# Causal attention with split-precision products: the scores run two tiles ahead of the transposes, and a tile's product stands behind the next tile's scores and transposes

## What is computed

```
x = x + attention(layernorm(x))
q, k, v = xn @ Wq.T, xn @ Wk.T, xn @ Wv.T               # 8 x 1024 x 256 each, one head
scores  = q @ k.T / 16, set to -inf above the diagonal
att     = softmax(scores)
attention = att @ v
```

## Time and profile before

| | |
|---|---|
| median of 3 runs | 2715.43 us (2697.62 to 2717.7) |
| the profiled execution's own time | 2705.96 us |
| span of the profile | 2703.8 us |
| the batches' tiles and projections, in the span | from 32 to 438 us, some 51 to 54 us a batch |
| busy over the span | PE 89%, PEld 82%, DVE 72%, ACT 44%, POOL 27% |

### The profile page before, as it was taken

How to read it: one execution, slowest core, us unless ns; L and a number is a source line. 1 busy time by engine, 2 the same in 40 slices (tenths; PEclk the granted TensorE clock), 3 DMA queues, 4 the chain that set the end, 5 groups by cost and what they waited for, 6 DMA issues and landing times. The chain is left out here.

```text
span 2703.8 us, 43605 instructions
## 1 busy us (share of the span) xinstructions
PE 2410.3 (89%) x15832; PEld 2204.0 (82%) x15832; DVE 1939.7 (72%) x3587; ACT 1180.7 (44%) x1834; POOL 732.7 (27%) x452
## 2 busy tenths in 40 slices
PE   6988896899899969999999999958888888799999
PEld 6887885888888858898898889847777777699998
DVE  5666665899999866467556656548999998766664
ACT  4344443434443325455456555523333333444444
POOL 1111011444444423122312302314434442211110
PEclk9999997999999989999999999968898989899999
DMA  5000000000000000000000000020000010100000
GB/s 168 0 0 0 0 0 19 1 1 0 0 0 0 1 16 1 16 8 8 16 12 8 12 16 8 9 67 24 17 24 16 16 39 2 41 19 21 23 23 32
DMA packets 43112, 45.91 MB, mean 17 GB/s; under 512 B 2976, under 2 KB 42016, under 8 KB 42784
## 3 DMA queue, kind: packets, MB, share of 16 engines
q1 hardware_dynamic: 43040, 44.95, 5.2%
HBM read 28.16 MB, written 16.78 MB: 17 GB/s over the span
## 5 line engine op out<-in xcount | busy, mean ns | idle before, releaser
L1777 ACT ACTIVATE m_a<-m_ps_wide,m_b 128x512 f32<-128x512 f32 x128 | 88.4, 690 | 286.3 <-PE m_ps_wide L271 202.1
L1745 PE MATMUL m_ps_z<-m_w_hi,m_a_hi 128*128 128x256 f32 x512 | 152.9, 299 | 52.8 <-DVE m_a_lo L1817 52.8
L1777 ACT ACTIVATE d_a<-d_ps_wide,d_b 128x512 f32<-128x512 f32 x128 | 88.3, 690 | 190.4 <-PE d_ps_wide L271 188.4
L1817 DVE TENSOR_TENSOR d_a_lo<-d_a,d_a_hi 128x512 fp32r<-128x512 f32 x128 | 86.8, 690 | 111.3 <-ACT d_a_hi L1781 110.4
L1269 POOL TENSOR_TENSOR p_kf<-p_kf,p_k_shift 128x1024 f32<-128x1024 f32 x64 | 119.5, 1904 | 155.3 <-DVE p_k_shift L1403 155.3
L1745 PEld LDWEIGHTS m_ps_z<-m_w_hi,m_a_hi 128*128 128x128 f32 x512 | 103.2, 202 | 66.7 <-DVE m_a_lo L1817 61.7
L1745 PE MATMUL m_ps_z<-m_w_lo,m_a_hi 128*128 128x256 f32 x512 | 150.1, 293 | 0.0
L1745 PE MATMUL m_ps_z<-m_w_hi,m_a_lo 128*128 128x256 f32 x512 | 149.9, 293 | 0.0
L1745 PE MATMUL d_ps_z<-d_w_hi,d_a_lo 128*128 128x256 f32 x512 | 145.4, 284 | 0.0
L1745 PE MATMUL d_ps_z<-d_w_lo,d_a_hi 128*128 128x256 f32 x512 | 145.0, 283 | 0.0
L1745 PE MATMUL d_ps_z<-d_w_hi,d_a_hi 128*128 128x256 f32 x512 | 143.9, 281 | 0.3 <-DVE d_a_lo L1817 0.3
(11 more groups left out here) (342 smaller groups left out, 8567.6 us busy)
## 6 DMA issues: line engine op xcount, KB each, us to landing
residual<-in_x SPq DMA_DIRECT2D x8, 1024.0 KB, 11.8
attn<-p_attn SPq DMA_DIRECT2D x32, 256.0 KB, 2.1
m_attn<-attn SPq DMA_DIRECT2D x16, 512.0 KB, 3.7
out<-residual SPq DMA_DIRECT2D x16, 512.0 KB, 2.9
raw_weights<-in_d_q SPq DMA_DIRECT2D x2, 1024.0 KB, 7.2
d_scale<-in_d_scale SPq DMA_DIRECT2D x2, 1024.0 KB, 6.3
raw_weights<-in_m_w1T SPq DMA_DIRECT2D x1, 1024.0 KB, 5.0
raw_weights<-in_m_w2T SPq DMA_DIRECT2D x1, 1024.0 KB, 9.4
```

What stands on the lines that cost most here:

```text
L1745: mm = pe.matmul(z, a, w[:, f, :], start=(f == 0 and k == 0 and j % 2 == 0), stop=(f == FC - 1 and k == 2), skip_group_check=True)
L1777: act.activation(self.a[f % RING][:, :], self.ps_wide[f % 2][:, :], self.func, bias=self.b1[:, f:f + 1])
L1817: dve.tensor_tensor(self.a2[1][:, f, :], self.a[f % RING][:, :], self.a2[0][:, f, :].bitcast(F32), ALU.subtract).then_inc(self.a_lo, 1)
```

## The change

```diff
         AHEAD = ["", "", "n0", "n1", "n2", "n3 n4", "n5 n6", ""]
-        TILES = ["", "", "s2 t0", "s3 w0 t1", "s4 w1 t2", "s5 w2 t3 w3 t4", "s6 w4 t5", "s7 t6 w5"]
+        TILES = ["", "", "s2 s3 t0 t1", "s4 w0 t2 w1", "s5 t3 w2", "s6 t4 w3", "s7 t5 w4", "t6 w5"]
         STEPS = {"s": "scores", "t": "turn", "w": "weigh"}
...
                 if what == "scores":
                     act.wait_ge(max_ready, b * TB + i + 1)
-                    if i in (4, 5):
-                        act.wait_ge(turned, probs_use(b, i - 2, 0) + 1)
+                    if i >= 4:
+                        act.wait_ge(turned, probs_use(b, i - 2, banks[i - 2] - 1) + 1)
                     at = first_bank(i) * BANK
```

## The result

Measured over 20 runs each, the changed kernel takes 2692.11 us (median, 2681.53 to 2704.43) and the kernel before 2707.94 us (2697.62 to 2723.57). The ratio is 0.9936 with a 95% interval of [0.9917, 0.9954], so the change gains 0.6%. The profiled execution took 2685.65 us (span 2683.4) against 2705.96 (span 2703.8). The attention layer, read by the first weight-scale reduction behind the last batch, ends at 418.73 us in place of 438.95, which is 20.2 earlier; what lies behind it takes 2264.7 in place of 2264.9. All of the difference between these two executions is in the layer.

The account below looks back on a forecast made before the run. TensorE, 89% busy, was taken as the bound, waiting in six places for a chain through ACT and DVE. 18 us of waits plus 7.5 of clock gave 2680.5 from 2705.96, ratio 0.991, so 2690 from 2715.43; range 2675 to 2706.

Parts of the forecast that it names:

- The waits, 18 us: Attention layer: TensorE's waits shrink, 2.2 us in six batches, 1.5 in the first, 3.1 in the last; 17.8, say 18.
- The clock, 7.5 us: Attention layer: 3 falls to half clock in place of 8, at 1.5 us each, gain 7.5 us.
- the one gap that I had named: TensorE's wait before t6 for the low part of t5, 2.05 us, the largest of the new batch.
- within 1%: Whole kernel: measured time within 1%, 27 us, of no change; chance 0.58.
- the chain takes the gain back: Rival: from tile 3 on the DVE and ACT chain sets the pace, costing 10 us; 2700 us, chance 0.12.
- the added wait would bind: Rival, slower: at exp6 and exp7 ACT waits for PE's transposes in a loop; gain gone or 2729 us, chance 0.03.
- No fall at all: Rival: no clock falls in the attention layer, 12 us back, 30 in all; 2685 us, chance 0.20.
- The rule on transposes: Skill's rule that transposes don't count as clock-gate activity; t6's gap would weigh at least as much, making 2697 us likelier.

Follow-up runs that it names:

- f1: The changed kernel with three slots of probs in place of two and without ACT's wait for transposes; 2680.88 us, 0.9873 of the kernel before.
- e1: Kernel before with only the early tiles reordered (s2 s3 t0 t1, s4 w0 t2 w1), later tiles as before; 2715.31 us, ratio 1.0006.
- e2: Kernel before with only the later tiles reordered (s5 t3 w2 s6 t4 w3, s7 t5 w4, t6 w5); 2693.24 us, 0.9937.
- copy first: The changed kernel, but ACT copies a tile's transposes ahead of the exponential beside them; 2651.88 us, 0.9785 of before; repeated 2652.89, 0.9782.
- its half: Only the later tiles reordered, early ones as before, with ACT copying ahead of the exponential; 2674.08 us, 0.9844 of the kernel before.

## Why the prediction came out as it did

**The waits, 18 us.** Right, to a microsecond. Walked: 0.8 inside t4, 0.45 before t5, 2.05 before t6, 1.05 before t7; measured with the 0.16 of overlap: 1.08, 0.52, 2.06 and 1.14. No wait before t0, w0, w1 and T0, as said; w2, walked as hidden by 0.2, loses 0.15. A clean batch was forecast at 49.0 to 49.1 and is 49.21. By parts: six ordinary batches 6 x 2.08 = 12.5 (forecast 13.2), the last one, its fall taken out, 3.4 (3.1), and the first from its tile-0 scores (31.89 before, 33.58 after) to its end, two falls taken out, 1.6 (1.5): 17.5 against 17.8. Part of the excess of the waits is a hand-over I had put at 0.04 and that is 0.11 where the exponential has the wait. Not all: without it (f1) the wait inside t4 is still 1.01 with the overlap, where 0.8 was walked.

**The clock, 7.5 us.** The mechanism was right, the size of the term was not. I took 3 falls for 8 and it was 5: three fewer and not five, a gain of 4.5 us and not 7.5. The five follow the one gap that I had named. The start of the kernel, which the sum put at nothing, took 1.7 us back: tile 0's scores start at 33.58 for 31.89. Ahead of every changed step the second eight transposes of the input last 1.94 us in the change and 1.07 before, and the first projection matmuls behind them are slower too; why is open. 17.5 + 4.5 - 1.7 = 20.3, which is the difference of the profiled executions.

**The median.** Forecast 2690, measured 2692.11. That the two lie so close is in part luck. The gain between the medians is 15.8 (20.3 between the profiled executions), well under the 25 of the forecast, and the median of before was 2707.94 over 20 runs and not the 2715.43 of three; the two errors cancel but for 2 us. The range, 2675 to 2706, holds it, and within 1% was the likeliest sign.

**The rivals.** That the chain takes the gain back is half true, and I had it as a mere lengthening. It had taken back the whole gain of the first half already: e1 and e2 show that. That the added wait would bind did not come about, its exponentials are released by the maximum; f1 shows that it costs 0.07 each time all the same. No fall at all, which the change itself did not bring, came true in every run whose longest gap in the layer was 1.82 as printed or less.

**The rule on transposes.** The Trainium skill, "TensorE: Matmul & The Clock Gate", Part 4, has transposes not count as activity for the clock gate (what it measured there was in bf16). The trace does not agree for these float32 transposes. Around t7 the changed kernel has T0 and T1 (eight transposes, from 314.32), a gap of 1.14 and eight more (from 316.33, about 0.1 each), 3.0 us (to w6 at 317.34) without one other matmul, and no fall follows there in any of seven batches, nor in the eight runs of mine that have the same steps there (in three of them, the two of copy first and its half, 0.5 of idle time stands before T0 too). The gap of 2.06 before t6 is followed by one in five of seven. In before, the same transposes with 2.1 of idle time about them had falls behind them in three of seven, in the first half alone in two of seven. By these rows the falls go with the idle time.

## What to carry to other kernels

When steps of a software pipeline are moved to cover a wait of one engine, write out the order of the helpers too: a copy that must free the next step should stand ahead of an operation that still waits for its own input, and work that nobody waits for (here statistics and normalisation) belongs where the helper idles anyway. Walk the new order against every engine's queue before counting a covered wait as a gain, since as long as a chain over the helpers sets the pace, what is saved early in it is waited for later. An order of ACT's own, with the other engines as in the change, gave the kernel 2.2% where the change gave 0.6%.

## What the runs showed of the hardware

A semaphore wait that is long satisfied still costs about 0.07 us when it is put ahead of an activation that has another wait, 0.11 against 0.04 from the end of the maximum to the start of the exponential, in the changed kernel against f1 and within the kernel before. TensorE's gaps of 3.6 us were followed by a clock fall in 7 of 7 batches (the first half alone), those of 2.45 in 5 of 8 (before), those of 2.06 in 5 of 7 (the change), and those of 1.98 (1.82 as printed, f1) and 1.75 (the second half) in none of 7 each. The step from 2.06 to 1.98 went with five falls, over 7 us; what tells the batches of one kernel apart is not shown. And one stretch of a layer that nobody touched was at either clock level in two executions of the same kernel, which cost 20 us there and left 10.7 between the spans.
